# Three edge aggregations of a graph network: sums held in PSUM per node tile instead of added into SBUF per window

## The reference

```python
# layer 0: 8 heads of 32, edges with attributes
attn = ex / jnp.maximum(denom[dst], 1e-10)
out = jax.ops.segment_sum(h_src * attn[..., None], dst, num_segments=n)
# layer 1: two attentions, first 4 heads of 128, then 1 head of 256
msg = h[src] * alpha[:, :, None]
out = jax.ops.segment_sum(msg, dst, num_segments=N)
```

## Time and profile before

| | us |
|---|---|
| three timed runs | 3231.08, 3237.75, 3236.89 |
| span of the profiled execution | 3241.8 |
| sum0, first to last matmul | 769.2 to 1037.2 |
| sum_h4, first gather to last add | 1775.0 to 2221.6 |
| sum_h1, first gather to last add | 2499.9 to 2901.1 |

### The profile page before, as it was taken

The page is one execution under the profiler, slowest core; times in us unless marked ns, Lnnn a source line. Parts: engine busy times, 40 slices in busy tenths (PEclk is TensorE's granted clock), DMA queues, the critical chain, the costliest instruction groups (busy, mean ns, idle before and its releaser), DMA issues. The chain is left out here.

```text
span 3241.8 us, 48906 instructions
## 1 busy us (share of the span) xinstructions
PE 2228.9 (69%) x10992; PEld 1503.4 (46%) x10993; DVE 2056.2 (63%) x3849; ACT 1246.0 (38%) x3616; POOL 1722.4 (53%) x1802
## 2 busy tenths in 40 slices
PE   3635777767997389948673899997661766654693
PEld 2322333335555356535562677776551444433341
DVE  7587777778788343452677788887682666665221
ACT  2223333326775221234001666665201666652010
POOL 1586777733554301132554777774466777751213
PEclk9867787778999599979766999998765899885555
DMA  4768888874885278825996788886896555530454
GB/s 140 205 181 231 260 263 262 261 235 138 218 219 161 96 254 278 263 90 197 364 396 196 243 274 269 273 276 166 240 291 175 148 147 149 146 107 23 132 152 132
DMA packets 456713, 668.49 MB, mean 206 GB/s; under 512 B 67154, under 2 KB 334092, under 8 KB 456001
## 3 DMA queue, kind: packets, MB, share of 16 engines
q1 hardware_dynamic: 334017, 357.96, 36.3%
q0 software_dynamic: 87248, 261.86, 27.3%
q10 hardware_dynamic: 35296, 46.90, 4.1%
HBM read 491.69 MB, written 176.23 MB: 206 GB/s over the span
## 5 line engine op out<-in xcount | busy, mean ns | idle before, releaser
L1533 POOL DMA_INDIRECT xn<-table,src_col x572 | 595.8, 1042 | 180.6 <-issue 148.9
L1574 PE MATMUL sum_h_ps<-xn,sum_h_hot 128*128 128x261 f32 (+1 forms) x1936 | 526.5, 415 | 192.0 <-DVE xn L1588 128.8
L1574 PEld LDWEIGHTS sum_h_ps<-xn,sum_h_hot 128*128 128x128 f32 x1936 | 369.7, 201 | 341.3 <-DVE xn L1588 251.6
L1092 POOL DMA_INDIRECT arena_a<-table,src_col x264 | 265.6, 1006 | 267.7 <-issue 184.7
L978 POOL DMA_INDIRECT arena_b<-table,src_col x336 | 318.7, 949 | 111.7 <-issue 108.6
L1588 DVE TENSOR_TENSOR xn<-xn,al 128x514 f32<-128x514 f32 (+1 forms) x352 | 243.4, 692 | 167.9 <-DMA xn<-table,src_col 164.0
L1597 DVE TENSOR_TENSOR arena_a<-arena_a,sum_h_ps 128x522 f32 (+1 forms) x440 | 246.1, 559 | 62.1 <-issue 38.2
L1707 PE MATMUL sum_ps<-xn,sum_hot 128*128 128x264 f32 x880 | 245.4, 406 | 31.4 <-DVE arena_a L1730 10.4
L1690 POOL TENSOR_TENSOR xn<-xn,al 128x264 f32<-128x264 f32 x220 | 158.8, 723 | 168.5 <-DMA xn<-edge_h 165.5
L1009 ACT ACTIVATE xn<-score_ps_en 128x512 f32<-128x512 f32 x220 | 131.4, 597 | 291.1 <-PE score_ps_en L995 287.4
L999 PE MATMUL score_ps_hd<-arena_a,score_hot 128*128 x1320 | 238.8, 330 | 0.0
(11 more groups left out here) (516 smaller groups left out, 4628.7 us busy)
## 6 DMA issues: line engine op xcount, KB each, us to landing
xn<-edge_h SPq DMA_DIRECT2D x220, 264.0 KB, 3.2
edge_h<-arena_b SPq DMA_DIRECT2D x84, 528.0 KB
arena_b<-kept SPq DMA_DIRECT2D x66, 516.0 KB, 5.4
xn_t<-edge_rows SPq DMA_DIRECT2D x110, 256.0 KB, 4.6
score_h_hot<-hots SPq DMA_DIRECT2D x220, 128.0 KB, 11.7
kept<-arena_a ACTq DMA_DIRECT2D x40, 516.0 KB, 9.1
xn<-kept SPq DMA_DIRECT2D x66, 257.0 KB
arena_a<-in_f_w SPq DMA_DIRECT2D x16, 1024.0 KB, 8.7
```

The costliest lines, as they stand in the source:

```text
L1092: pool.indirect_dma_start(rows[:, q, s, :], None, table, bass.IndirectOffsetOnAxis(ap=K.src_col[:, w * SUB + s:w * SUB + s + 1], axis=0)). ...
L1533: pool.indirect_dma_start(rows[w][:, s, 0:RW], None, table, bass.IndirectOffsetOnAxis(ap=K.src_col[:, w * SUB + s:w * SUB + s + 1], axis=0 ...
L1574: ins = pe.matmul(ps[:, u, b, 0:part], lhsT=hot[:, w % QH, s, :], rhs=rows[w][:, s, b * part:(b + 1) * part], start=(s == 0), stop=(s == S ...
```

## The change

All three aggregations keep a node tile's sum in a PSUM bank for as long as its windows last. The bank is `tile mod 8` (`mod 4` pairs of banks in sum_h4). Its number, and the number of tiles that must have been emptied before, are two tables in SBUF (`K.bank`), and TensorE loads four entries of each into registers once every four windows (`load_four`, L147 of the new kernel). All matmuls run with `start=False`. The banks are cleared once by matmuls with zeros at the start of a stage. ACT waits for a tile's last window (`K.tile_end`), copies the bank to `acc` and clears the bank, 25 times in a stage. DVE's adds, its register loads and the clearing of `acc` are gone. DVE now makes every one-hot, as two TENSOR_SCALAR of 128x128 per window in place of one TENSOR_TENSOR of 128x256. In `aggregate` it makes both subtiles' messages in one instruction, and copies the extra columns; ACT does none of this any more. POOL's and SyncE's parts stay as they were. `items_project_l0` gets six more small DVE instructions, each waited for.

TensorE in sum0, a window of the loop before; L1703 is the wait for the one-hot, L1707 the two matmuls of a window.

```diff
+def load_four(engine, values, low, high):
+
+    return engine.bass.values_load_multi_w_load_instructions(values, engines=(engine.engine,), min_val=low, max_val=high)[1]
...
             step(dve.tensor_copy(K.window[:, :], t_f[:, :]))
+            step(dve.tensor_scalar(K.bank[:, 0, :], K.window[:, :], 1, None, ALU.add))
+            step(dve.tensor_scalar(K.bank[:, 1, :], K.window[:, :], BANKS - 1, None, ALU.bitwise_and))
+            step(dve.tensor_scalar(K.bank[:, 2, :], K.window[:, :], BANKS // 2 - 1, None, ALU.bitwise_and))
+            step(dve.tensor_copy(key_i[:, :], key_t[:, :]))
+            step(dve.tensor_scalar(K.tile_end[:, 0:NT - 1], key_i[:, :], EB.bit_length() - 1, None, ALU.logical_shift_right))
+            step(dve.memset(K.tile_end[:, NT - 1:NT], W))
...
@@ aggregate
         def _(act):
-            def one_hot(w):
...
+            act.wait_ge(s_none, 1)
+            for t in range(NT):
+                end = act.value_load(K.tile_end[0:1, t:t + 1], min_val=1, max_val=W)
+                act.wait_ge(s_sum, end + QH)
+                act.activation(acc[:, t, :].rearrange("p (b c) -> p b c", b=B), ps[:, t % SLOTS, :, 0:part], ACT.Copy).then_inc(s_out, 1)
+                act.wait_ge(s_out, t + 1)
+                if t + SLOTS < NT:
+                    act.activation(ps[:, t % SLOTS, :, 0:part], none[:, :, :], ACT.Copy).then_inc(s_free, 1)
         def _(pe):
...
+            for u in range(SLOTS):
+                for b in range(B):
+                    ins = pe.matmul(ps[:, u, b, 0:part], lhsT=K.ident[:, :], rhs=none[:, b, :], start=True, stop=True)
+            ins.then_inc(s_free, SLOTS)
             for w in range(W):
-                u = w % U2
-                pe.wait_ge(s_ready, per_ready * (w + 1))
-                pe.wait_ge(s_act, min(2 * W, 2 * (w + 1) + AHEAD) if by_act else 2 * (w + 1))
-                if w >= U2:
-                    pe.wait_ge(s_acc, w - U2 + 2)
+                if w % 4 == 0:
+                    needs = load_four(pe, K.bank[0:1, 0, w:w + 4], 1, NT)
+                    banks = load_four(pe, K.bank[0:1, B, w:w + 4], 0, SLOTS - 1)
+                pe.wait_ge(s_hot, w + 1)
+                pe.wait_ge(s_msg, 2 * (w + 1))
+                pe.wait_ge(s_free, needs[w % 4])
...
         def _(dve):
             def message(i, j):
                 w = i * J + j
+                dve.wait_ge(s_sum, w + 1)
+                for s in range(SUB):
+                    ins = dve.tensor_scalar(hot[:, j % QH, s, :], K.iota_row[:, :], K.rel_col[:, bass.ds(w * SUB + s, 1)], None, ALU.is_equal)
+                ins.then_inc(s_hot, 1)
                 sem, at, per_turn = landed[j]
                 dve.wait_ge(sem, i * per_turn + at)
+                dve.tensor_copy(rows[j][:, :, RW:RW + X], extra[:, bass.ds(w * SUB, SUB), :]).then_inc(s_msg, 1)
+                view = rows[j][:, :, 0:RW].rearrange("p s (h r) -> p s h r", h=H)
+                dve.tensor_tensor(view, view, al[:, bass.ds(w * SUB, SUB), :].unsqueeze(3).broadcast_to([P, SUB, H, RW // H]),
+                                  ALU.mult).then_inc(s_msg, 1)
...
-            dve.memset(acc, 0.0).then_inc(s_acc, 1)
+            dve.memset(none[:, :, :], 0.0).then_inc(s_none, 1)
...
```

More of the change, by code:

```diff
@@ L62 @@
 KQ = 5
+BANKS = 8
 EARLY0 = 26
@@ L1495, in aggregate @@
         hot = st.sbuf("hot", [P, QH, SUB, P])
-        ps = st.psum("ps", [P, U2, B, 512])
+        none = st.sbuf("none", [P, B, part])
+        ps = st.psum("ps", [P, SLOTS, B, 512])
         s_gath, gathered = K.gath, list(K.gathered)
         s_rows = [st.sem(f"rows{q}") for q in range(QS)]
[L1499 to L1504, removed]
+        s_none, s_hot, s_msg, s_sum, s_free, s_out, s_pad = (st.sem(n) for n in ("none", "hot", "msg", "sum", "free", "out", "pad"))
         direct = [w for w in range(W) if w not in STAGED]
@@ L1604, in _ @@
+            dve.memset(none[:, :, :], 0.0).then_inc(s_none, 1)
             turns = W // J
-            with aligned(dve, 0, turns - 1) as i:
+            with aligned(dve, 0, turns) as i:
                 for j in range(J):
-                    message(i + (j + 2) // J, (j + 2) % J)
-                    add(i, j)
-            for j in range(J):
-                if j + 2 < J:
-                    message(turns - 1, j + 2)
-                add(turns - 1, j)
-            dve.wait_ge(s_acc, W + 1)
+                    message(i, j)
@@ L1629, in aggregate_l0 @@
         rows = K.xn[:, :, :].rearrange("p t d -> p (t d)")[:, 0:Q * SUB * ROW0].rearrange("p (q s r) -> p q s r", q=Q, s=SUB)
-        by_dve = [j for j in range(J) if j % 5 == 4]
-        by_act = [j for j in range(J) if j not in by_dve]
-        made = {j: n for n, j in enumerate(by_act)}
         hot = st.sbuf("hot", [P, Q, SUB, P])
-        away = st.sbuf("away", [P, 2, SUB, P])
-        one = st.sbuf("one", [P, 1])
-        ps = st.psum("ps", [P, U2, 512])
-        s_zero = st.sem("zero")
+        none = st.sbuf("none", [P, ROW0])
+        ps = st.psum("ps", [P, BANKS, 512])
+        s_none = st.sem("none")
         s_rows = [st.sem(f"rows{q}") for q in range(Q)]
-        s_one, s_away, s_hot, s_hot2, s_msg0, s_msg1, s_sum, s_acc = (st.sem(n) for n in ("one", "away", "hot", "hot2", "msg0", "msg1", "sum", "acc"))
+        s_hot, s_msg0, s_msg1, s_sum, s_free, s_out = (st.sem(n) for n in ("hot", "msg0", "msg1", "sum", "free", "out"))
         turns = W // J
@@ L1713, in message @@
                 w, q = i * J + j, j % Q
+                dve.wait_ge(s_sum, w + 1)
+                for s in range(SUB):
+                    ins = dve.tensor_scalar(hot[:, q, s, :], K.iota_row[:, :], K.rel_col[:, bass.ds(w * SUB + s, 1)], None, ALU.is_equal)
+                ins.then_inc(s_hot, 1)
                 dve.wait_ge(s_rows[q], 16 * (i * (J // Q) + j // Q + 1))
```

133 lines of the change are left out of this document (34 added, 99 removed).

## The result

The changed kernel takes 3295.64 us (median of four runs, 3289.09 to 3298.11) against 3237.32 before: 1.0182 times as long, 95% interval 1.0168 to 1.0197, or 58 us more. The forecast was 3271 us, with a range of 3185 to 3335. Its profiled execution has a span of 3296.2 us, 54.4 more than the one of before.

The account below looks back on a forecast made before the run. POOL's gathers were taken to bound sum_h4 and sum_h1, with sum0 near DVE's 1.17 us a window. Terms +32.4, +9.3, -8.4 and +1.0 make +34.3 on 3236.9, so 3271 us, range 3185 to 3335.

Parts of the forecast that it names:

- sum_h4, forecast +32.4: sum_h4: longer messages raise the excess per gather from 0.135 to 0.28 us, +44.7, less 12.8, plus 0.5 us.
- first gather -12.8: Start of sum_h4: without the clearing of `acc` the first gather takes 0.95 us in place of 13.75.
- The prediction's formula: sum_h4 and sum_h1: with random starts, an instruction L per window T adds L x L / 2T a gather; 0.31 us in sum_h4.
- sum_h1, +9.3 forecast: sum_h1: excess 0.065 us a gather against 0.030, +10.8 us, less 1.5 at the start.
- sum0, -8.4 forecast: sum0: 1.18 us a window, 259.6 us against 268.0; ends -50 and +29.
- the sign, gaps on PE every fourth window: sum0: the new profile would show gaps on PE every fourth window; no size given.
- The loads in sum_h4, costed at nothing: TensorE in sum_h4: register loads run on the sequencer while queued matmuls run, so they add 0 us.
- The one-hots beside the gathers: sum_h1: DVE's 440 fp32 TENSOR_SCALARs of 128 columns might block gathers, allowed for inside 0.03 us of excess.
- Elsewhere, +1.0 forecast: `items_project_l0`: six more DVE instructions, 1.5 us, partly beside an awaited DMA; +1.0 us, between 0 and 2.
- A: Rival, faster: gathers settle between messages, excess 0.135 us in sum_h4, sum0 at 1.05 a window; 3187 us, chance 0.26.
- B: Rival, no change: excess 0.19 us in sum_h4 (+4.6), +3 in sum_h1, -8.4 in sum0; 3237 us, chance 0.08.
- C: Rival, much slower: backlogged DVE holds every gather, 0.39 us in sum_h4, sum0 at 1.28 a window; 3353 us, chance 0.12.

Follow-up runs that it names:

- mixed: Changed kernel with one register load per four windows, TENSOR_TENSOR one-hots in sum0, TENSOR_SCALAR messages in sum_h1 and for subtile 0 of sum_h4: 3247.64 us.
- split: Changed kernel with the message of sum_h4 as two back to back TENSOR_TENSORs of 516 elements in place of one of 1032: 3301.60 us.
- split_apart: Changed kernel with the message of sum_h4 as two TENSOR_TENSORs of 516 elements and the window's one-hots between them: 3279.60 us.
- sum0_tt: Changed kernel with DVE's one-hots of sum0 as one TENSOR_TENSOR a window in place of two TENSOR_SCALARs, both register loads kept: 3289.32 us (one run).
- one_load: Changed kernel with one TensorE register load per four windows in place of two in all three stages, the bank computed by register arithmetic: 3263.26 us.
- ts_msg: Changed kernel with messages of sum_h4 and sum_h1 by TENSOR_SCALARs, one per subtile and head, in place of one TENSOR_TENSOR: 3282.88 us.
- before_ts: Kernel before the change with DVE's messages of sum_h4 and sum_h1 by TENSOR_SCALARs: 3209.16 us, ratio 0.9921.

## Why the prediction was right, point by point

**sum_h4, forecast +32.4, measured +33.6.** The mechanism of the hold and the sizes of the terms held: excess 0.284 us a gather (0.28 taken), first gather -12.8 (0.95 for 13.75), tail +0.3 (7.9 against 7.6 us behind the last gather; 0.5 was taken). The first gather's term is right in size alone: the prediction put it to the clearing, and what that gather waited for stays open. The size of the excess was partly luck. The prediction's formula gave 0.31 and its own ratio for sum_h4 0.39; the 0.28 was chosen between the ends, and no row gave it. The lock, in which 109 of the 308 gathers are held, was not seen. mixed, where the same formula gave 0.11 and the chip 0.265, shows how far it can be off.

**sum_h1, +9.3 forecast, +2.9 measured.** An excess of 0.045 us in place of 0.065, near the lower end: in this stage DVE waits before the copy in 132 of the 220 windows, nearly always for a landing. Of the +2.9 little can be said. Three further kernels with the same sum_h1 code, split, split_apart and sum0_tt, took 403.5, 408.2 and 406.9 us there, 2.3 to 7.0 above before, which itself was profiled once.

**sum0, -8.4 forecast, +15.2 measured.** This step failed, by its sign, and 23.6 us of error are here. The prediction had the price of the loads, "0.5 to 0.9 us a window for loads beside what it does now", and compared it with the array. It never added the two parts of the sequencer: 0.82 us of loads and 0.43 of waits and dispatch, 1.25 a window, above the 1.18 that was taken. sum0_tt and one_load show that nothing else sets it. It did name the sign, gaps on PE every fourth window, without adding up what they cost. DVE's window was too short as well. Two one-hots are 0.47 us and 0.84 beside POOL, not 0.30, which one_load made visible as the next bound.

**The loads in sum_h4, costed at nothing.** The cost is right, since one_load leaves the stage at 483.6 us, but the reason given is not. The prediction had the loads run under queued matmuls, and would have called itself wrong if PE's gaps followed them. They do follow them:

```profile
PEld sum_h_ps L1573 <- issue: 90.1, 73, 4.7
```

Of 62 gaps of more than 0.5 us between weight loads in sum_h4, 45 stand at the start of a group of four windows, 65.8 of 84.9 us. They cost nothing because POOL is the bound and TensorE has the time. In one_load 22 gaps of 20.5 us are left there, others have grown in their place (79.1 us in all), and the stage is no shorter.

**The one-hots beside the gathers, up to 0.03 us taken.** They are fp32 tensor_scalars of 128 elements. In the changed kernel's sum_h1, 144 gathers start under one, with an excess of 0.013 us on average. With 440 of them and 1760 like messages in ts_msg's sum_h4, the mean gather is 0.975 us. The Trainium skill ("SBUF — State Buffer", "Who interferes with whom") counts tensor_scalar among the instructions that can block GpSimd in a 2-port mode, and reports that tensor_tensor did not stall descriptor generation in its probe. On tensor_scalar the traces agree, as the gathers under L2184 and L2186 show, but the hold ends with the instruction, and one of 128 elements is too short to matter. On tensor_tensor the indirect gathers of this kernel differ from that probe, and the measurement decides. That two engines share one path in SBUF agrees with sum0: a one-hot takes 438 ns beside POOL's TENSOR_TENSORs and 280 in sum_h4.

**Elsewhere, +1.0 forecast.** +0.8 ahead of sum0; the table is not to be told from the scatter.

**The other rivals.** A (gathers settle between the messages) did not come: the two engines settle on each other. B and C lie on either side of what was measured.

Open: what holds the first gather of sum_h4 before, why a pair of TENSOR_TENSORs sometimes holds to its end and mostly does not, and why sum_h4 keeps landing in the dear phase and sum_h1 in the cheap one.

## What to carry to other kernels

Indirect gathers are held by a long instruction of VectorE with two tensor inputs in SBUF, and by a long TENSOR_SCALAR too. Short TENSOR_SCALARs by a per-partition scalar leave gaps, but take VectorE longer: eight took 1.65 us where one TENSOR_TENSOR took 1.23, and they paid only where VectorE had that time (before_ts, and not sum_h4 of ts_msg). Look at the gathers' mean time and not only at who waits. Before registers are loaded on an engine, add up that engine's sequencer, loads and dispatch together, and compare the sum with the stage's period. If an engine is held and released by another in a loop, expect the two to lock, and read the phase from the timeline; an average over random starts can be far off (0.11 against 0.265 us in mixed).

## What the runs showed of the hardware

- A gather that starts under a TENSOR_TENSOR with two SBUF inputs ends 0.82 us behind its end, at 516 and at 1032 elements, if that is later than its own 0.946 us; in mixed the same holds for gathers that start 0.05 us ahead of it. Of two back to back, 34 gathers of 95 waited for the second (2106.57 against 2105.75) and 57 for the first alone.
- Under a TENSOR_TENSOR with one input in PSUM a gather is not held: 57 start under L1597 in sum_h4 of the kernel before, and the longest excess is 0.01 us.
- A TENSOR_SCALAR of 1280 elements (0.83 us) holds a gather until 0.81 to 0.85 us behind its end. With TENSOR_SCALARs of 128 and 129 elements the mean gather is 0.975 us in sum_h4 (0.946 undisturbed), and under back to back MEMSETs of 522 it is 0.95.
- A register load of four values on TensorE takes 1.5 to 1.6 us of its sequencer: 0.33 for the load, 0.28 for each value and its bounds, and the steps between.
- 25 MEMSETs of 522 elements take 0.493 us each, 12.3 together, and one of 13050 takes 10.93: the pieces cost 1.4 us more of DVE and freed 12.8 of POOL.
